# Last pass of a gated cross-attention kernel: half of the row gathers made plain with the addition on VectorE, six stages in another order, and the last group's heads added by VectorE

## The reference

```
x = x + jnp.tanh(g_xattn[0]) * _L0_xattn_ref(_layernorm(x, axis=-1), ctx_1024, ctx_1024, ...)
x = x + jnp.tanh(g_ffn[0]) * _L0_ffn_ref(_layernorm(x, axis=-1), L0_ffn_wg, L0_ffn_w1, ...)
x = x + jnp.tanh(g_xattn[1]) * _L1_xattn_ref(_layernorm(x, axis=-1), ctx_1024, ctx_1024, fside_1xSxS2_0, ...)
x = x + jnp.tanh(g_ffn[1]) * _L1_ffn_ref(_layernorm(x, axis=-1), L1_ffn_CB, L1_ffn_SCB, L1_ffn_bias)
```

```
qk = jnp.einsum('bqd,bkd->bqk', qp, kp) * scale
qk = qk + mask
attn = jax.nn.softmax(qk, axis=-1)
return jnp.einsum('bqk,bkd->bqd', attn, v1)
```

## Time and profile before

| | |
|---|---|
| median of 3 executions | 569.85 us (569.83 to 570.12) |
| the profiled execution's own time | 571.48 us |
| its span | 569.7 us |
| TensorE busy | 506.6 us, 89% |
| VectorE busy | 333.4 us, 59% |
| ScalarE busy | 306.9 us, 54% |
| GpSimd busy | 217.3 us, 38% |
| mean granted TensorE clock | 0.88 |

### The profile page before, as it was taken

One profiled execution on the slowest core, in us unless ns is written; L12 is line 12 of the kernel. 1 busy time (PEld: TensorE's weight loads), 2 busy tenths in 40 slices (PEclk: granted clock), 3 DMA queues, 4 the chain that ended last, 5 costly groups with the idle time before them and its releaser, 6 DMA issues. The chain is left out here.

```text
span 569.7 us, 13049 instructions
## 1 busy us (share of the span) xinstructions
PE 506.6 (89%) x3926; PEld 366.2 (64%) x3926; DVE 333.4 (59%) x1455; ACT 306.9 (54%) x764; POOL 217.3 (38%) x210
## 2 busy tenths in 40 slices
PE   3589999999999999998889999999975788888886
PEld 2566787887777778774437777777732356656563
DVE  6345788877877778688423223333112677877873
ACT  4666666656666656422123333333204578888873
POOL 4301124434444445466700000000058888888500
PEclk9997778778777767698789999999995999999999
DMA  4973112222222111140121444443143556666621
GB/s 119 224 197 86 58 58 76 77 76 76 74 74 74 56 35 40 40 130 24 51 68 45 112 112 111 111 111 93 38 110 37 113 108 144 135 145 144 138 76 55
DMA packets 85068, 52.00 MB, mean 91 GB/s; under 512 B 7555, under 2 KB 78886, under 8 KB 85030
## 3 DMA queue, kind: packets, MB, share of 16 engines
q1 hardware_dynamic: 73766, 43.09, 27.7%
q0 software_dynamic: 11264, 8.43, 8.6%
HBM read 26.07 MB, written 16.91 MB: 75 GB/s over the span
## 5 line engine op out<-in xcount | busy, mean ns | idle before, releaser
L692 POOL DMA_INDIRECT s_xs<-slots_y,s_gidx x64 | 98.8, 1544 | 152.5 <-DMA slots_y<-s_ye 133.2
L822 ACT ACTIVATE s_ht<-heads,s_cols 128x512 f32<-128x512 f32 x64 | 44.0, 687 | 82.7 <-PE heads L1079 82.4
L147 ACT ACTIVATE s_xn<-s_xs,s_ln_shift,s_ln_rstd 128x128 f32 (+1 forms) x192 | 77.6, 481 | 15.6 <-DVE s_ln_shift L140 15.5
L669 POOL DMA_INDIRECT slots_x<-s_xn,s_sidx x56 | 55.1, 984 | 56.8 <-DVE s_sidx L1376 44.0
L99 DVE BATCH_NORM_STATS2 s_ln_stats<-s_xs 128x6 f32 (+1 forms) x256 | 54.5, 279 | 25.8 <-DMA s_xs<-slots_y,s_gidx 20.3
L1079 PE MATMUL heads<-s_xet,s_w_sb 128*128 128x512 f32 x128 | 59.4, 608 | 1.7 <-DVE s_xet L1456 1.7
L1086 PE MATMUL bank<-s_w_sb,s_ht 128*128 128x128 f32 x512 | 59.9, 275 | 0.9 <-DVE s_ye L1465 0.9
L1086 PEld LDWEIGHTS bank<-s_w_sb,s_ht 128*128 128x128 f32 x512 | 58.5, 192 | 1.5 <-issue 1.5
L656 POOL TENSOR_TENSOR s_hs<-s_hs,s_head_w 128x512 f32<-128x512 f32 x16 | 20.3, 1268 | 95.4 <-DVE s_hs L1337 95.4
L968 PE MATMUL heads<-s_dec_r,s_dec_l 128*128 128x512 f32 x64 | 52.5, 970 | 1.7 <-DMA s_dec_r<-s_mrow 1.7
L911 PE MATMUL bank<-s_ones_b 128*128 128x512 bf16 x187 | 50.4, 410 | 0.0
(11 more groups left out here) (195 smaller groups left out, 954.2 us busy)
## 6 DMA issues: line engine op xcount, KB each, us to landing
slots_x<-s_xe SPq DMA_DIRECT2D x8, 516.0 KB, 7.8
s_xe<-slots_x SPq DMA_DIRECT2D x16, 258.0 KB, 3.2
s_xs<-in_x_dram SPq DMA_DIRECT2D x16, 256.0 KB, 3.0
s_ctxb<-in_ctx_dram SPq DMA_DIRECT2D x16, 256.0 KB, 3.2
s_kpt<-s_kt SPq DMA_DIRECT2D x16, 256.0 KB, 2.7
s_w_sb<-in_L_ffn_w_dram SPq DMA_DIRECT2D x16, 256.0 KB, 3.3
slots_y<-s_ye SPq DMA_DIRECT2D x16, 256.0 KB, 2.3
s_ctxv<-in_ctx_dram SPq DMA_DIRECT2D x16, 256.0 KB, 3.5
```

Of the source, the lines that this page charges most:

```text
L147: last = act.activation(out(t), tile(t), ACT.Identity, bias=self.shift[:, j:j + 1], scale=self.rstd[:, j:j + 1])
L669: pool.indirect_dma_start(out=slots_x, out_offset=bass.IndirectOffsetOnAxis(ap=slots_of(g, q)[:, t:t + 1], axis=0), in_=routed(g)[:, q, t, ...
L692: pool.indirect_dma_start(out=xs[:, n * D:(n + 1) * D], out_offset=None, in_=slots_y, in_offset=bass.IndirectOffsetOnAxis(ap=gidx[:, n:n + ...
L822: act.activation(ht[:, s_par, c, :], heads[:, c, :], ACT.Gelu_apprx_tanh, bias=col).then_inc(h_done, 1)
```

## The change

In the last pass, the first two tiles of a group are gathered as before, with the addition in the DMA. The other two are gathered plainly into `yg`, a view of the buffer `ex`, which is idle in this pass, and one VectorE instruction (`add_rows`) adds them to `xs`. A gather of group g now waits for that addition in group g-2. The pipeline of the pass has six stages on all engines: the third norm stands in step g instead of g+1 (counted by `over_groups`), and the outputs still in step g+5. The statistics and moments of the two norms are split (`dve_part`, `dve_variances`): those of the fourth norm are taken at the end of the step before. Keys and values are loaded apart (`load_k` up to six groups ahead, `load_v` up to five). `keep_clock` issues two matmuls ahead of every `turn_rows4`, and no others in the pass. In the first pass VectorE does the two instructions of `add_heads` for group 15.

```diff
+    def dve_part(self, dve, i, g, tile):
+        self.dve_stats(dve, i, tile)
+        hold(dve, self.stats_done[i], g + 1, self.go)
+        for t in range(GT):
+            last = dve.bn_aggr(self.mv[:, i * GT + t, :], self.stats[:, i * GT + t, :])
+        last.then_inc(self.part_done[i], 1)
+
+    def dve_variances(self, dve, parts):
+        for i, g in parts:
+            hold(dve, self.part_done[i], g + 1, self.go)
...
+            def load_k(g, q):
+                hold(sp, s3_ps, g - 1, consts)
+                sp.dma_start(kpr[:, q, :], kpt[:, bass.ds(g * GW, GW)]).then_inc(kpr_in[q], 16)
...
             def add_heads(g, half, q):
+                if isinstance(g, int) and g == NG - 1:
+                    return
...
             def gather(g):
-                need(pool, ln34.stats_done[0], g - 1)
+                need(pool, y_added, g - 1)
                 for t in range(GT):
                     n = g * GT + t
-                    pool.indirect_dma_start(out=xs[:, n * D:(n + 1) * D], out_offset=None, in_=slots_y,
-                                            in_offset=bass.IndirectOffsetOnAxis(ap=gidx[:, n:n + 1], axis=0),
-                                            compute_op=ALU.add).then_inc(yg_in[g % 2], 16)
+                    if t < ADDED:
+                        pool.indirect_dma_start(out=xs[:, n * D:(n + 1) * D], out_offset=None, in_=slots_y, in_offset=rows_at,
+                                                compute_op=ALU.add).then_inc(yg_in[g % 2], 16)
+                    else:
+                        pool.indirect_dma_start(out=yg[:, g % 2, t - ADDED, :], out_offset=None, in_=slots_y,
+                                                in_offset=rows_at).then_inc(yg_in[g % 2], 16)
...
             def last_pass(at):       # ScalarE
-                one, two, three, four, five = at
+                zero, one, two, _, four, five = at
+                if two:
+                    probabilities(*two)
+                if one:
+                    queries3(*one)
+                if norms:
+                    ln34.act_guess(act, k, norms)
                 if five:
                     rows4(*five)
+                if two:
+                    turned_probabilities(*two)
+                if one:
+                    projected_queries(*one)
+                if zero:
+                    ln34.act_apply(act, k, 0, lambda t: xn3[:, t, :], xtile(zero[0]))
+                if four:
+                    ln34.act_apply(act, k, 1, lambda t: xn4[:, t, :], xtile(four[0]))
...
             def turn_rows4(g, half, q):
-                keep_clock(6, 3 if not isinstance(g, int) or g < NG - 2 else 6 if g < NG - 1 else 11)
+                keep_clock(6, 2)
...
             def last_pass(at):       # TensorE
+                if one:
+                    turn_queries3(*one)
                 if five:
                     turn_rows4(*five)
+                if two:
+                    turn_probabilities(*two)
+                if one:
+                    project_queries(*one)
                 if five:
                     product4(*five)
+                if one:
+                    scores3(*one)
+                if two:
+                    values3(*two)
...
+            def add_rows(g, half, q):
+                hold(dve, yg_in[q], half * (16 * GT) + 16 * GT, consts)
+                late = xs[:, bass.ds(g * GW + ADDED * P, GW - ADDED * P)]
+                dve.tensor_tensor(late, late, yg[:, q, 0:GT - ADDED, :].rearrange("p t d -> p (t d)"), ALU.add).then_inc(y_added, 1)
```

More of the change, by code:

```diff
@@ L82, in __init__ @@
         self.mv_done = sem(f"{name}_mv_done")
+        self.part_done = [sem(f"{name}_part_done{i}") for i in range(2)]
         self.ve_done = sem(f"{name}_ve_done")
@@ L581, in _ @@
                 sp.wait_ge(keys_kept[q], 16 * NG // 2)
[L582 to L585, removed]
-                for q in range(2):
[L587 to L592, removed]
+            load_k(0, 0)
+            load_k(1, 1)
+            load_v(0, 0)
+            load_v(1, 1)
+            for g in range(2, KEYS_AHEAD):
+                load_k(g, g % 2)
+                if g < VALUES_AHEAD:
+                    load_v(g, g % 2)
+            with sp.Fori(0, (NG - KEYS_AHEAD) // 2) as half:
+                for q in range(2):
+                    store(half * 2 + q, q)
+                    load_k(half * 2 + q + KEYS_AHEAD, (q + KEYS_AHEAD) % 2)
+                    load_v(half * 2 + q + VALUES_AHEAD, (q + VALUES_AHEAD) % 2)
+            for g in range(NG - KEYS_AHEAD, NG):
+                store(g, g % 2)
+                if g + VALUES_AHEAD < NG:
+                    load_v(g + VALUES_AHEAD, (g + VALUES_AHEAD) % 2)
             for q in range(2):
@@ L1185, in last_pass @@
             def last_pass(at):
-                one, two, three, four, five = at
-                if four:
-                    turn_probabilities(*four)
-                if three:
-                    project_queries(*three)
-                if four:
-                    values3(*four)
-                if three:
-                    scores3(*three)
+                _, one, two, _, _, five = at
+                if one:
+                    turn_queries3(*one)
                 if five:
@@ L1414, in first_pass @@
                     scaled_heads(*four)
+                    if isinstance(four[0], int) and four[0] == NG - 1:
+                        add_last_heads(four[0], four[2])
                 if three:
@@ L1521, in last_pass @@
             def last_pass(at):
[L1522 to L1537 removed]
+                zero, _, two, three, four, five = at
+                norms = [(i, here[0]) for i, here in enumerate((zero, four)) if here]
+                if two:
+                    score_maxima(*two)
+                if zero:
+                    add_rows(*zero)
+                    hold(dve, y_added, zero[0] + 1, consts)
+                    ln34.dve_part(dve, 0, zero[0], xtile(zero[0]))
+                if norms:
+                    k = step_of(at)
+                    ln34.dve_variances(dve, norms)
+                if three:
+                    attention_sums(*three)
+                    add_attention(*three)
                 if norms:
@@ L1540, in last_pass @@
                     ln34.dve_shift(dve, k, norms)
[L1541 to L1542 removed]
                 if three:
[L1544 to L1546 removed]
+                    hold(dve, x3_done, three[0] + 1, consts)
+                    ln34.dve_part(dve, 1, three[0], xtile(three[0]))
+                if five:
+                    outputs(*five)
             over_groups(dve, NG, 6, last_pass)
```

65 lines of the change are left out of this document (22 added, 43 removed).

## The result

The changed kernel takes 563.47 us (median of 4 runs, 563.20 to 566.33), beside 569.99 for the kernel before on the same chip. The ratio is 0.9886, interval 0.9853 to 0.9918: faster by 1.1%. I had forecast 564.0 with a range of 560.2 to 568.8.

The account below looks back on a forecast made before the run. Gather supply (7.40 us a group) and a three-engine chain (about 7.5) bound it together. Group 0 at 427.7, four steps of 6.8, 11 of 7.2, then 20.4, 7.9 and 1.4 gave span 563.8, median 564.0, range 560.2 to 568.8.

Parts of the forecast that it names:

- Two limits, supply and chain: Last pass: gather supply of 7.40 us a group and a three-engine chain of about 7.5 set the step together.
- Why the waits for TensorE go: VectorE's step: waits of 0.38 and 0.84 us go, since maxima and attention sums stand a whole step behind their matmuls.
- Plain gather: GpSimd's last pass: a plain gather takes 0.97 us, with 0.30 ahead of it, making a group 6.24.
- Rival 1: Last pass: a plain gather costs what the adding one does, supply stays 7.40, median 571.3 us; chance 0.10.
- Head: Start of the last pass: ScalarE's third norm of group 0 at 427.7 us, then four steps of 6.8 to 454.9.
- VectorE's step: Last pass, groups 5 to 15: 6.34 + 0.46 + 0.21 + 0.2 = 7.2 us a step, 79.2 for 11.
- Rival 4: Last pass: the new order leaves waits on VectorE, step near 7.4, 566 to 567.5 us; chance 0.12.
- Rival 3: Last pass: VectorE's row addition and GpSimd's gathers shut each other out, 0.8 us a step, 572.5; chance 0.04.
- First pass, 0.95: End of first pass: group 15's heads on VectorE end a stall, all later times 0.95 us earlier.
- Tail, 20.4: End of last pass: the last group's four steps to its fourth norm take 6.5, 5.4, 4.8 and 3.7, together 20.4 us.
- The end: From the last fourth-norm activations to the span's end: 7.9 us, plus 1.4 for TensorE's clock falling once.
- Rival 2: Last pass: TensorE's clock falls inside the loop, 3.7 us for each slow step, median 579; chance 0.06.

Follow-up runs that it names:

- experiment 1: The kernel before with two plain gathers in four and the row addition on VectorE, in the old order: 582.14 us, ratio 1.0114.
- experiment 2: The changed kernel with all four gathers adding and no row addition on VectorE: 570.93 us, ratio 0.9931 to the kernel before.
- experiment 6: The changed kernel with VectorE's last pass written out group by group instead of looped: 557.13 us, ratio 0.9718 to the kernel before.
- experiment 5: The changed kernel run again, unaltered: 565.47 us, ratio 0.9860 to the kernel before.
- experiment 10: The changed kernel without filler matmuls in the last pass and with VectorE's last pass written out: 556.45 us, ratio 0.9741 to the kernel before.
- experiment 4: The changed kernel without the two filler matmuls ahead of each turn of the fourth norm's rows: 577.11 us, ratio 1.0044 to the kernel before.
- experiment 11: The changed kernel with the last heads back on GpSimd and VectorE's last pass written out: 555.60 us, ratio 0.9712 to the kernel before.

## Why the prediction was right, and where its terms were off

- **Two limits, supply and chain.** Shown by experiments 1 and 2: each half alone keeps the limit that the other one lifts. That it takes both is the main reason why the forecast held.
- **Why the waits for TensorE go.** They went, but not for the reason given. The maxima do not stand a whole step behind their scores: the score matmuls end only 0.5 to 0.6 ahead of them. Only for the attention sums is there room (2.3 to 2.7). With half a microsecond less on VectorE the wait would be near, as experiment 6 shows; that it was covered is in part luck.
- **Plain gather, 0.97 taken.** Measured 985 ns as the mean of 32. Rival 1 is refuted. A group's supply is 6.36 in the profile (416.21 to 422.57), forecast 6.24.
- **Head.** Group 0 at 427.26 (forecast 427.7), group 4 at 455.16 (454.9). The middle value for the steps, 6.8, was 6.98 from the earlier start.
- **VectorE's step, the mis-sized term.** Forecast 7.2, measured 7.37. The row addition is 0.42 to 0.43 (forecast 0.46) and the splits are what the rows gave. What was too small, as far as the rows show, is the 0.2 for three more waits against a register. I took half of a visible wait for it; in the changed kernel the pieces around the row addition alone are 0.20 in every step and 0.16 in each second, and that ahead of L128 is 0.28 in each second. The 11 steps took 80.05, 0.85 more than forecast. The larger thing that I didn't see is the loop form as a whole: 0.8 a step in the changed kernel, by experiments 5 and 6. Some of it must have been in the 6.34 of before already, whose list has idle pieces of 0.17 and 0.21 too; how much, no run shows, since the loop of before was not written out.
- **Rival 4** gave a step near 7.4, and the step was 7.37. But the waits that it named aren't there; its number was nearly met by another cause.
- **Rival 3** is refuted in its size, 0.8 a step, but not wholly. The row addition at 443.95 lasted 0.42 inside the gather that starts at 443.33, which took 1.54 as ever. A gather that starts just behind the start of a row addition is longer, though. From experiment 10, VectorE's and GpSimd's rows:

```profile
488.77 0.42 DVE L1538 TENSOR_TENSOR s_xs<-s_xs,s_ex 128x256 f32<-128x256 f32 x1
```

```profile
488.81 1.24 POOL L728 DMA_INDIRECT s_ex<-slots_y,s_gidx  x1 [0.30 <-issue]
```

Over all traces the 15 plain gathers that start 0.04 to 0.17 behind the addition's start take 1.25 to 1.10, one that starts 0.23 behind it 1.06, and from 0.28 on 0.97 to 1.01. In the profile after that happened once (1.11 at 471.67), so it cost next to nothing. The Trainium skill ("SBUF — State Buffer", "Who interferes with whom") says that a VectorE instruction with two SBUF inputs contends with a GpSimd instruction that reads SBUF. The stretch of 1.6 us under GpSimd's own addition, in the earlier trace rows, is what it describes; for gathers the trace agrees only at their start, with up to 0.25 us.

- **First pass, 0.95.** Measured 1.0 from the scaled heads to the transposes, in every trace. The profile after shows 1.61 at the last scatter (281.61 against 283.22); 0.44 of it was there before the edited place was reached (262.32 against 262.76), and 0.2 came behind the transposes, in a stretch whose length changes between executions (see the last section). Both are outside the change and were in no term.
- **Tail, 20.4.** Measured 18.83 (535.21 to 554.04): the four steps took 6.27, 5.29, 4.09 and 3.18, forecast 6.5, 5.4, 4.8 and 3.7. The last two, with the least work, were overrated most.
- **The end.** From the last norms 7.96, forecast 7.9. The 1.4 for a fallen clock did not come: it stayed at 1.00 to the end. It did come in experiment 10, without any fillers, and cost 0.9 there. Rival 2 did not come either.
- **The load split, nothing.** No run tests it alone. In the last pass of the profile after TensorE has no wait for a load, which fits.

The errors of the loop (+0.85) and of the head (+0.7, less 0.44) stand against tail (-1.6) and clock (-1.4): the forecast of 563.8 for a span that came to 562.0 is in part a balance of errors. A further error brought the median closer. The profiled execution was 1.5 above the median before (571.48 against 569.99), which the prediction took to stay, and is 0.25 above it after (563.72 against 563.47). So the span fell by 7.7, 1.8 more than forecast, and the median by 6.5, only 0.6 more. That the time came within 0.5 of the forecast is in part luck.

## What to carry to other kernels

When two limits stand within a few per cent of each other, test each half of a change alone: one half here costs 1.1%, the other (with the last heads) gives 0.7%, together they give 1.1 to 1.4%. Before reordering for tenths of a microsecond, write out the loop of the engine that bounds: that gave another 1.4% here with no change of the work. Price a small edit by the distance between two rows close around it, in several traces, not by the total of the kernel.

## What the runs showed that was not expected

- **VectorE's loop form costs 0.8 us in a step of 7.4**, in pieces of 0.16 to 0.28 that the profile gives to issue or to VectorE's own last result. The Trainium skill, "Runtime: NRT & Kernel Launch", section "Instruction fetch mechanics", gives fetch stalls at taken branches as one reason why runtime control flow is expensive and kernels prefer unrolling. The gain agrees in direction, but no run here shows a fetch stall. Every second step is longer (7.20 and 7.57 in turn between ScalarE's norms; the body holds two groups). In VectorE's list the two groups of a body differ by 0.13 of idle time ahead of the row addition and 0.18 ahead of L128, both inside a step, and by 0.15 ahead of the maxima, where one step meets the next and a branch can stand. Most of the 0.8 lies between instructions of one body, where waits against registers stand.
- **A second, slower pace of the same loop.** Two edits that leave VectorE's loop as it is brought steps of 8.2 to 8.3, with 0.6 to 0.9 idle ahead of the maxima; written out, both run at 6.5 to 6.6. So the loop form is needed for it. What VectorE waits for there is open: the named matmul had the same distance as in the kernel without the gap. A wait that is just missed could be the reason, or where code lies for the fetch; experiment 4 leaves VectorE's own list untouched, which speaks against the second. No run here separates them.
- **The end of the first pass varies from execution to execution.** With the heads on VectorE it takes 19.3 us from the scaled heads to the last scatter in three traces and 21.1 to 21.3 in seven; with them on GpSimd 20.5, 22.1, 23.5 and 23.7. That is more than many an edit gives. The mean granted clock of the stretch doesn't order them: the kernel before has the lowest, 0.75 from 262 to 285 us, and 20.5, experiment 11 has 0.78 and 22.1. It matters where the low level (0.50) lies. In the profile after and in experiment 10 the eight fillers ahead of the last group's transposes are these:

```profile
270.55 1.90 PE L946 MATMUL bank<-s_ones_b 128*128 128x512 bf16 x8
```

```profile
270.66 3.59 PE L946 MATMUL bank<-s_ones_b 128*128 128x512 bf16 x8
```

They take 3.5 to 3.6 in six of the seven long traces, and 1.90 in the three short ones. The seventh, experiment 2, has 1.90 too; so its length has another reason, which isn't shown.
